# Order of steps in a four-layer attention stage: the last group's norms in the first beats, and the last beat's old result and Gelu table

## What is computed

```python
h = _L0_tok_ref(x, itok, itok, ...)                  # embedding
h = h + _L0_attn_ref(_layernorm(h), ...)             # phase attention
h = h + _L0_ffn_ref(_layernorm(h), ...)              # 8 experts, top 2
h = h + _L1_attn_ref(_layernorm(h), ...)             # four layers, below
h = h + _L1_ffn_ref(_layernorm(h), ...)              # 8 experts, top 2

def _forward(x, ...):                                # inside _L1_attn_ref
    for i in range(4):
        h = _layernorm(x, ln1_g[i], ln1_b[i])
        x = x + _linear_attn(h, Wq[i], Wk[i], Wv[i], Wo[i], bo[i])
        h = _layernorm(x, ln2_g[i], ln2_b[i])
        x = x + (gelu(h @ W1[i] + b1[i]) @ W2[i] + b2[i])
    return x
```

## Time and profile before

| what | value |
|---|---|
| median of 3 runs | 550.0 us (548.64 to 551.19) |
| the profiled execution | 547.61 us |
| its span, first to last instruction | 545.9 us |
| TensorE busy in the span | 497.7 us (91%) |
| VectorE, ScalarE, GpSimd busy | 388.7, 367.7, 64.0 us |
| chain that ended last, by engine | PE 71%, DVE 14%, ACT 11% |

### The profile page before, as it was taken

How to read it: one execution, slowest core, us unless ns; L and a number is a source line. 1 busy time by engine, 2 the same in 40 slices (tenths; PEclk the granted TensorE clock), 3 DMA queues, 4 the chain that set the end, 5 groups by cost and what they waited for, 6 DMA issues and landing times.

```text
span 545.9 us, 8929 instructions
## 1 busy us (share of the span) xinstructions
PE 497.7 (91%) x3126; PEld 260.0 (48%) x3126; DVE 388.7 (71%) x954; ACT 367.7 (67%) x614; POOL 64.0 (12%) x82
## 2 busy tenths in 40 slices
PE   1998999999999999678999999999968999999995
PEld 0565685444433333445556665666544335333331
DVE  5877897696546758777999999999884357623444
ACT  0368737846756664356998999899956765666651
POOL 3000001200000000021432343234201000000000
PEclk9989998999999999978999999999999999999999
DMA  6920200411211221300000000000000412223221
GB/s 210 276 37 2 58 2 1 120 55 62 83 59 58 77 79 41 114 1 1 1 2 2 2 1 1 2 1 1 2 2 14 128 56 79 59 82 95 80 74 42
DMA packets 26300, 28.14 MB, mean 52 GB/s; under 512 B 11184, under 2 KB 16848, under 8 KB 26192
## 3 DMA queue, kind: packets, MB, share of 16 engines
q1 hardware_dynamic: 23408, 26.85, 17.1%
q10 hardware_dynamic: 2848, 0.71, 0.7%
HBM read 26.24 MB, written 1.31 MB: 50 GB/s over the span
## 4 chain that ended last, share of the span: by engine, by line
PE 71%; DVE 14%; ACT 11%; issue 3%; DMA 1%; SPq 0%; DVEq 0%; ACTq 0%
PE banks L1658 20%; PE banks L1670 20%; ACT Hd L820 6%; PE banks L1772 4%; PE banks L1850 4%; PE banks L1829 3%; PE banks L1841 3%; PE banks L1793 3%; PE banks L1494 2%; PE banks L1806 2%; DVE Mm L1354 1%; PE banks L1532 1%; DVE Ph L1123 1%; DVE mom L983 1%; PE banks L1817 1%
## 5 line engine op out<-in xcount | busy, mean ns | idle before, releaser
L722 ACT ACTIVATE Hd<-banks,b1all 128x512 f32<-128x512 f32 x128 | 76.1, 703 | 35.5 <-PE banks L1658 35.3
L722 ACT ACTIVATE Ph<-banks,b1all 128x512 f32<-128x512 f32 x128 | 75.8, 704 | 31.7 <-PE banks L1658 31.7
L1214 DVE SCALAR_TENSOR_TENSOR Tmp<-banks,b2col,Wb 128x512 f32<-128x512 f32 x56 | 42.0, 750 | 71.3 <-PE banks L1670 69.6
L1658 PE MATMUL banks<-Ph,w1m 64*128 64x512 f32 x256 | 61.5, 618 | 0.3 <-ACT Ph L708 0.3
L1658 PE MATMUL banks<-XT,w1m 64*128 64x512 f32 x256 | 60.4, 605 | 0.0
L1670 PE MATMUL banks<-Hd,w2m 128*64 128x512 f32 x256 | 58.9, 599 | 0.0
L1670 PE MATMUL banks<-Ph,w2m 128*64 128x512 f32 x256 | 58.4, 598 | 0.0
L592 POOL TENSOR_TENSOR l1stat<-l1stat,power 128x8 f32<-128x8 f32 x28 | 46.2, 1650 | 2.3
L820 ACT ACTIVATE Hd<-banks,lvecs 128x512 f32<-128x512 f32 x60 | 36.5, 688 | 6.1 <-PE banks L1841 6.1
L1218 DVE TENSOR_TENSOR Rest<-Rest,Tmp 128x512 f32<-128x512 f32 x56 | 38.8, 692 | 1.9
L1658 PEld LDWEIGHTS banks<-XT,w1m 64*128 64x128 f32 x256 | 26.0, 186 | 28.7 <-issue 25.1
(11 more groups left out here) (223 smaller groups left out, 853.2 us busy)
## 6 DMA issues: line engine op xcount, KB each, us to landing
Wb<-gate_rows SPq DMA_DIRECT2D x128, 128.0 KB, 2.9
Ph<-in_x SPq DMA_DIRECT2D x4, 512.0 KB, 8.4
Ph<-in_itok SPq DMA_DIRECT2D x4, 384.0 KB, 9.1
w1m<-in_w1e SPq DMA_DIRECT2D x1, 1028.0 KB, 17.3
w2m<-in_w2e SPq DMA_DIRECT2D x2, 512.0 KB, 13.2
w1m<-in_w1e SPq DMA_DIRECT2D x1, 1024.0 KB, 5.5
out<-Hs SPq DMA_DIRECT2D x14, 64.0 KB, 2.1
Hd<-in_w1all SPq DMA_DIRECT2D x1, 512.0 KB, 13.4
```

Source lines behind the costliest of these rows:

```text
L722: read(ac.activation(hidden_of(st)[:, k // 2, k % 2, :], ps(key)[:, :], func, bias=b1all[:, st.m, st.e, k // 2:k // 2 + 1]), key)
L1214: ve.scalar_tensor_tensor(dst, bank[st.down_bank][:, :], b2, Wb[:, st.t % RING, :], ALU.add, ALU.mult).then_inc(down_read, 1)
L1658: made(te.matmul(dst[:, :], w1m[hs, st.e, k // 2 * P:(k // 2 + 1) * P], operand[hs, gslice(st.g)], start=True, stop=True), key)
```

## The change

Five moves, none of which adds or removes an instruction of arithmetic. On VectorE `norm_centre(4, 3, Hs)` (with its wait) goes behind beat 0's mix, `norm_scale(4, 3, Xs)` behind beat 1's mix, and `first_norms(3)` in beat 2 in front of the queries' maximum. In beat 15 of VectorE, `fed_out` and `finished` of job 13 go in front of the keys' sum and the mix of job 15. In beat 16, ScalarE loads Gelu's table in front of everything, and TensorE turns job 13's result back (`yt`) in front of the queries' transposes and the mix of job 15. The name `fed` at the end of VectorE's program becomes `prev`, since `fed` is now a function.

```diff
@@ ScalarE, beat(t)
                 if now:
                     rows_out("xa", now, 0)
+                if t == JOBS:
+                    ac.preload_act_table(ACT.Gelu)
                 if feed:
                     rows_out("xf", feed, 2)
                 if old:
@@
                 if feed:
-                    ac.preload_act_table(ACT.Gelu)
+                    if now:
+                        ac.preload_act_table(ACT.Gelu)
                     hidden_out(feed)
@@ VectorE
+            def fed(job):
+
+                fed_out(job)
+                if job.last:
+                    l1_taken(dve, "yt", job)
+                    finished(job.g)
+
@@ VectorE, beat(t)
                     centre(attn, 1, attn.ring, attn.done)
+                if t == 2:
+                    first_norms(3)
                 if now:
                     queries_max(now)
@@
                 if t == 0:
                     mixed(0, 3)
-                if t == 2:
-                    first_norms(3)
                 if old:
                     scaled(old, 0, old.done)
@@
                     context_out(now)
+                if t == JOBS - 1:
+                    fed(feed)
+                if job_at(t + 1, 0):
+                    keys_max(job_at(t + 1, 0))
+                if now:
+                    keys_sum(now)
+                    mix_out(now)
                 if t == 0:
                     taken(dve, ("at", 0, 3))
                     norm_centre(4, 3, Hs)
                 if t == 1:
                     norm_scale(4, 3, Xs)
-                if job_at(t + 1, 0):
-                    keys_max(job_at(t + 1, 0))
-                if now:
-                    keys_sum(now)
-                    mix_out(now)
-                if feed:
-                    fed_out(feed)
-                    if feed.last:
-                        l1_taken(dve, "yt", feed)
-                        finished(feed.g)
+                if feed and t < JOBS - 1:
+                    fed(feed)
@@ TensorE, beat(t)
                 if last:
                     context(t, last)
+                if old and t == JOBS:
+                    l1_taken(pe, "fdown", old)
+                    turn(t, "yt", Yt[:, old.ring, :])
                 if now:
                     keys(t, now)
                 if last:
                     pe.wait_ge(qn_ready, last.done)
                     turn(t, "qt", Qe[:, last.g, :])
                     mix(t, last)
-                if old:
+                if old and t < JOBS:
                     l1_taken(pe, "fdown", old)
                     turn(t, "yt", Yt[:, old.ring, :])
```

More of the change, by code:

```diff
@@ L1453, in _ @@
             layernorm(5, 0, Hs, Xn)
-            fed, tail = Job(JOBS - 2), Job(JOBS - 1)
-            fed_out(fed)
+            prev, tail = Job(JOBS - 2), Job(JOBS - 1)
+            fed_out(prev)
             attended_out(tail)
@@ L1458, in _ @@
             centre(tail, 1, tail.ring, tail.done)
-            l1_taken(dve, "yt", fed)
-            finished(fed.g)
+            l1_taken(dve, "yt", prev)
+            finished(prev.g)
             scaled(tail, 1, tail.done)
```

## The result

| what | before | after |
|---|---|---|
| median of the runs | 548.58 us (22 runs) | 550.62 us (22 runs) |
| most of them lie within | 546.18 to 551.25 | 547.64 to 553.85 |
| the profiled execution | 547.61 us | 547.83 us |
| its span | 545.9 us | 546.1 us |

The ratio is 1.0038, with an interval from 1.0020 to 1.0057: within 0.5% of no change, and 1.1 to 3.1 us above it. (One disturbed run of each kernel, 593.2 and 565.07, lies outside the second line.) The profiled execution of after is among its shortest: the profiles differ by 0.2 us, the medians by 2.0. So the trace gives the places of the change, and the runs have to say how often each place looks like that.

What follows compares the result with a forecast made beforehand. The chain was taken to run through VectorE's mix in the four-layer stage's last beat, then TensorE's expert matmuls. Head -2.04 and tail +2.18 gave +0.14 on 547.61, 547.75; adding 2.4 from profile to median gave 550.1 us, range 547.4 to 552.7.

Steps and rivals of the forecast that it cites:

- a sign of being wrong: Prediction wrong if beat 16's attention came no later, the 2 us were gone by beat 4, or these clocks differed.
- Head, step 1: VectorE, beat 0: centring goes behind the mix, so job 0's attention sum comes 1.02 us earlier, bound by VectorE.
- Head, steps 2 and 3: VectorE, beats 1 and 2: scaling behind the mix, first norm before the queries; head in all -2.04 us.
- the rival of a clock that stays up: TensorE, head: less idling keeps the clock up, -0.75 to -2.3 us, 547.8 to 549.3; chance 0.14.
- step 3: VectorE, beat 2: group 3's first norm before the queries fills idle time; beat 3's transposes at 248.87 instead of 250.91.
- the last rival: Head: norm before the queries delays the shift and values' copy, losing all the gain; 552.2 us, chance 0.08.
- Last beat, order: Beat 16: early table load, job 13's turn and adds delay job 15's mix and attention; +2.18 us.
- the cover: Beat 16, ScalarE: the table load was free before, as Gelu had nothing to read; moved, it has nothing covering it.
- the 551.5 us: Forecast time if the skill's drain of about 1380 ns were added to the table switch, tail 3.6 us; not counted.
- the first rival: TensorE, beat 16: clock falls in the wait for the turn, 1.56 to 3.1 us, 551.7 to 553.2; chance 0.16.
- the head's rival: TensorE, beats 1 to 3: clock stays up, gaining 0.75 to 2.3 us; chance 0.14.

Runs made afterwards that it cites:

- the whole change with TensorE filled in the last beat: Whole change plus four unread matmuls on TensorE in beat 16, three behind job 15's context, one before its attention; 547.74 us, ratio 0.9979 to before.
- the last beat's moves with filling: Kernel before with only the last beat's moves, plus four unread matmuls on TensorE in beat 16; 552.26 us, ratio 1.0027 to before.
- the table late: Whole change, but the last beat's Gelu table loaded directly in front of the Gelus, as before; 549.21 us, ratio 0.9989 to before.
- the norms' moves and the early table: Kernel before with the three norm moves and, of the last beat's moves, only Gelu's table in front; 547.33 us, ratio 0.9961 to before.

## Why the prediction was right, and where it was not

The forecast was 550.1 us and no change by over 0.5%; 550.62 and 1.0038 came. As an effect I forecast +0.14 us, and the runs show +2.0. That the time agrees to half a microsecond is luck: the 550.1 was built on a median of 550.0 for before, from three runs, and 22 runs beside the change give 548.58. Behind the effect stand two errors of opposite sign, both in the clock; that the granted clock would differ in beats 1 to 3 or 16 I had named as a sign of being wrong, and it came.

**Head, step 1: right.** The attention sum of job 0 went from 229.72 to 228.48, or 1.07 us with the 0.17 of the start taken off; 1.02 was forecast, with VectorE as what is late next, and no idle time stands ahead of the row.

**Head, steps 2 and 3: right in order, wrong in size.** In the whole change with TensorE filled in the last beat, job 2's keys' matmul ran at the low clock, as in before, and everything came as worked out. Less the 0.64 by which its first copy of values stood later than before's, its rows give 246.50 for the queries' maximum (forecast 246.59) and 248.81 for the transposes (forecast 248.87):

```profile
235.50 2.08 PE L1802 MATMUL banks<-XT,bdk 128*128 128x512 f32 x2
...
247.14 0.68 DVE L1317 TENSOR_REDUCE small<-banks 128x64 f32<-128x512 f32 x1
...
249.45 1.94 PE L1781 MATMUL banks<-ident,Xn 128*128 128x128 f32 x8 [3.26 <-ACT Vt L790]
```

There the head gained 2.10 us; the forecast was 2.04. In the profile of after the keys' matmul ran at full clock and the head gained 3.67: the rival of a clock that stays up, worth 1.6 more. What step 3 was said to bring, 1.18 of the 2.04, was not in it where the clock is up: the queries' operands come early there, the norm delays them by its 2.90 us, and the copy of the values becomes the wait. This is the mechanism of the last rival. The prediction named it, but its sum only asked whether the operands could come later than in before, not what a clock that stays up would make of them.

**Last beat, order: right.** +2.18 us, to the hundredth: from the copy of the keys to the down-projection 2.57 (forecast 2.56), to the turn 3.30 (3.31), to the mix 5.52 (5.52). Where I costed the cover, one wait was missing that happened not to be the last: the bank shared by job 14's rows and job 15's queries. It decides once the turn is not moved (0.60 us).

**The table load: the trace held.** The copy ahead of it ends at 390.87 + 0.58 = 391.45, the load runs from 391.47 to 392.75, and the rows follow at 392.76. There is no room for the further 1380 ns that the Trainium skill (ScalarE: Activation LUTs, "What ACT_TABLE_LOAD costs") adds to each switch, and the 551.5 us that followed from it were not needed for the result.

**The clock in the last beat: the step that failed.** I wrote "I take nothing, since the row nearest to the tail, the slices that hold beat 16, shows the high clock". That row showed a beat in which TensorE idles 0.88 us; the change makes it idle 1.99 and 0.96, by my own reckoning. After such a change the old slice is no row for the new one. The price was bounded at 1.56 to 3.1, and it was 2.06 us in after's profile; by the medians, filling takes 2.9 off. It was the first rival's mechanism, at a chance of 0.16: it was there in after's profile and gone in the profile with filling. The 1.8 us that every run of the last beat's moves has beyond the order would fit it, but no experiment places them.

In the profiled run the head's rival came true with it, -1.63 there against +2.06 here, and so the sum stayed near nothing. In the medians the parts add up like this: the norms' moves alone give -3.06, the order of the last beat +2.18, together -0.88; the whole change with filling shows -0.84, and without filling +2.04. So by the medians, too, there are two errors of opposite sign: the head gives 1.0 us more than forecast, and the clock of the last beat, put at nothing, takes 2.9. That -0.88 and -0.84 agree so closely is chance, as each interval is some 2 us wide to either side.

**Profile and median.** That the profiled run lies 2.4 us under the median, as I added it, held for neither kernel: it is 1.0 in before and 2.8 in after, whose profiled run is one of four at 0.984, the highest mean clock of its 22. These four took 547.64 to 548.33 us, the 17 of before at 0.984 or more 547.12 to 548.02, 0.5 apart by their medians. That is near the +0.14 of the sum, but in the profiled run, one of them, two errors of some 2 us cancel. In the runs at 0.976 to 0.983 the medians are 550.34 and 548.46.

What stays open: where the runs of the last beat's moves with filling lose their time, 10 of 12 being long; why the low clock comes early in the fifth stage in four profiles and not in the others; how large step 3's effect is with the clock down; and whether filling adds to steps 1 and 2.

## What to carry to other kernels

An order worked out step by step from rows was good to 0.1 us at six places here; what it can't give is the clock at which the moved work will run, so where an edit lengthens TensorE's idle time, the low clock belongs into the sum and not only into the range. Test it apart: unread matmuls in the idle time add no dependence, and on the whole change they separated the price of the order (6.05 with and without them) from the price of the clock. They are no sure remedy: on the last beat's moves alone most runs stayed long, and on before the time came back as low clock in the fifth stage. And move as few steps as carry the gain: centring and scaling behind the mixes gave all of it (0.9925), the first norm in front of the queries nothing more that these runs can show (0.9937), and the moves of the last beat took it back.

## What the runs showed of the hardware

- TensorE's clock fell to 1.2 GHz in the last beat of after 0.9 us behind a wait of 1.99 us, and in the longest run with the table late during a wait of 1.28, which came behind one of 0.57; it stayed at 2.4 GHz behind a wait of 0.88 in before and behind one of 1.50 with the norms' moves and the early table. So in these runs the length of the last wait alone doesn't tell whether it falls. It stayed low for 6.5 us in after, although TensorE was busy for 5.54 of them. The Trainium skill (TensorE: Matmul & The Clock Gate, "What's actually happening") says that the monitor runs free of the kernel's start, so that equal kernels meet it at different points; that one kernel's runs lie between 541.67 us at a mean clock of 0.993 and 548.85 at 0.973 is in line with it, but no run here shows the monitor itself.
- Work that nobody reads made one kernel, the whole change, shorter: the three matmuls behind the context (six records) fill 1.56 us of otherwise idle time, a fourth stands in front of the attention, and the median is 2.9 us below that of the change without them.
